# First experts: weights as the stationary operand, 256 gathered rows as the moving one

## The reference, cut to what matters

```python
logits = xf @ router_w + router_b                 # 4096 tokens, 4 experts
probs = softmax(logits)
top_p, top_i = top_k(probs, 2)                    # two experts for each token
gates = top_p / sum(top_p), scattered to [T, 4]
h = silu(einsum('td,edf->etf', xf, w1)) * einsum('td,edf->etf', xf, w3)   # D 256, F 1024
expert_out = einsum('etf,efd->etd', h, w2)
out = einsum('te,etd->td', gates, expert_out)
```

## Time and profile before

| | |
|---|---|
| median of 3 runs | 1969.44 us (1968.93 to 1970.89) |
| the profiled execution | 1968.24 us |
| its span in the trace | 1966.5 us |
| TensorE busy | 1695.0 us, 86% of the span |
| VectorE, GpSimd, ScalarE busy | 1152.6, 1051.4, 861.2 us |
| first experts, from the first `turn` to the copy of the last `down` | 514.18 to 1117.03 us |

### The profile page before, as it was taken

How to read it: one execution, slowest core, us unless ns; L and a number is a source line. 1 busy time by engine, 2 the same in 40 slices (tenths; PEclk the granted TensorE clock), 3 DMA queues, 4 the chain that set the end, 5 groups by cost and what they waited for, 6 DMA issues and landing times.

```text
span 1966.5 us, 32279 instructions
## 1 busy us (share of the span) xinstructions
PE 1695.0 (86%) x11144; PEld 1031.1 (52%) x11144; DVE 1152.6 (59%) x1838; ACT 861.2 (44%) x1932; POOL 1051.4 (53%) x871
## 2 busy tenths in 40 slices
PE   5699999977899999999999747788879676999992
PEld 3355555554466666666666523334434244677771
DVE  7799888976423232323323396999999986122224
ACT  3444444325344444443444356444444344444443
POOL 3377777623133333332444399999997954223322
PEclk8699999985799999999999967999999875999995
DMA  5012233106432233223343340011111355111115
GB/s 215 1 43 97 97 107 108 44 16 224 163 94 85 82 95 95 91 76 95 95 158 100 121 128 1 1 38 36 29 26 56 113 171 180 39 41 44 44 39 177
DMA packets 114424, 170.48 MB, mean 87 GB/s; under 512 B 27985, under 2 KB 78177, under 8 KB 114145
## 3 DMA queue, kind: packets, MB, share of 16 engines
q1 hardware_dynamic: 104096, 140.61, 21.1%
q0 software_dynamic: 10176, 27.80, 5.4%
HBM read 105.19 MB, written 63.18 MB: 86 GB/s over the span
## 4 chain that ended last, share of the span: by engine, by line
PE 64%; DVE 14%; POOL 10%; issue 6%; DMA 3%; ACT 3%; SPq 0%; DVEq 0%; POOLq 0%; ACTq 0%
PE ps L657 56%; POOL BIG L2014 9%; DVE BIG L1139 7%; PE ps L928 5%; DVE BIG L1596 2%; ACT BIG L1661 1%; PE ps L900 1%; DMA BIG<-YT 1%; DVE X L1139 1%; DVE bnst L1146 1%; DMA HB<-BIG 1%; PE ps L772 1%; POOL BIG L2135 1%; PE ps L832 1%; POOL X L2014 1%
## 5 line engine op out<-in xcount | busy, mean ns | idle before, releaser
L657 PE MATMUL ps<-BIG 128*128 (+9 forms) x8100 | 1301.8, 336 | 132.9 <-DVE BIG L1574 45.5
L657 PEld LDWEIGHTS ps<-BIG 128*128 128x128 f16 (+2 forms) x8100 | 739.1, 104 | 603.8 <-issue 114.9
L2014 POOL TENSOR_TENSOR BIG<-BIG 128x512 f16<-128x512 f32 (+5 forms) x530 | 765.4, 1478 | 261.2 <-ACT BIG L1661 242.3
L1139 DVE TENSOR_TENSOR BIG<-ps,BIG 128x512 f32<-128x512 f32 (+4 forms) x693 | 464.3, 724 | 271.1 <-ACT BIG L1661 225.4
L1661 ACT ACTIVATE BIG<-ps 128x512 f16<-128x512 f32 (+5 forms) x1036 | 396.7, 440 | 514.0 <-PE ps L657 264.8
L2109 POOL DMA_INDIRECT YT<-BIG x106 | 105.1, 992 | 541.8 <-ACT BIG L1661 541.8
L1139 DVE TENSOR_TENSOR BIG<-BIG,ps 128x512 f32<-128x512 f32 (+1 forms) x204 | 120.9, 597 | 414.7 <-PE ps L657 399.1
L1661 ACT ACTIVATE BIG<-BIG 128x512 f16<-128x512 f32 (+2 forms) x321 | 197.0, 630 | 133.4 <-DVE BIG L1139 98.8
L1815 ACT ACTIVATE BIG<-ps 128x512 f32<-128x512 f32 x212 | 126.8, 598 | 135.1 <-PE ps L657 135.1
L1596 DVE TENSOR_REDUCE BIG<-BIG 128x160 f32<-128x2560 f32 x64 | 183.5, 2868 | 0.0
L2104 POOL DMA_INDIRECT BIG<-HB,BIG x106 | 103.2, 974 | 69.7 <-DVE BIG L1139 43.7
(11 more groups left out here) (129 smaller groups left out, 857.6 us busy)
## 6 DMA issues: line engine op xcount, KB each, us to landing
WD<-BIG SPq DMA_DIRECT2D x112, 256.0 KB, 2.3
BIG<-in_v SPq DMA_DIRECT2D x32, 512.0 KB, 5.1
BIG<-WD SPq DMA_DIRECT2D x32, 512.0 KB, 5.0
BIG<-in_w SPq DMA_DIRECT2D x24, 512.0 KB, 3.9
BIG<-WD SPq DMA_DIRECT2D x32, 384.0 KB, 7.5
BIG<-YT SPq DMA_DIRECT2D x24, 512.0 KB, 4.9
HB<-BIG SPq DMA_DIRECT2D x64, 128.0 KB, 2.3
X<-in_x SPq DMA_DIRECT2D x4, 1024.0 KB, 11.7
```

Of the source, the lines that this page charges most:

```text
L657: return e.matmul(o, lhsT, rhs, start=start, stop=stop, skip_group_check=True)
L1139: return e.tensor_tensor(o, a, b, op)
L2014: return e.tensor_tensor(o, a, b, op)
```

## The change

In the first layer's experts, groups of 256 rows take the place of tiles of 128: 8192 / 256 + 3 = 35 groups (`NG`), which is 70 tiles of 128 for gathers, scatters and the down product. `up(j, g)` makes 256 inner features (two blocks of 128) for 256 rows in one bank: the weight's 128 columns are the stationary operand, at the register's address, and the 256 turned rows in `HTT` are the moving one. Inner features come out on partitions, so `turn_up` is gone: ScalarE's `up_hi` and VectorE's `up_lo` make the f16 pair straight from `UP` in SBUF. `UP` is now two buffers of 512 and `up` number u waits for `up_lo` of u - 2. `HIN` has four buffers, both gathers of a group are fetched before it, and the turned rows are copied 1024 wide. The second layer's experts keep their form (the code is split in two functions).

```diff
-                self.NS = CH * NT + E - 1
+                self.rows = 256 if l == 0 else 128
+                self.NG = CH * NT * 128 // self.rows + E - 1
+                self.NS = self.NG * self.rows // 128
...
-                self.HIN = area.ring(3, 2 * D, dt=f16)
-                self.HTT = area.ring(2, 4, 128, dt=f16)
-                self.UP = area.ring(2, 1024)
-                self.UPT = area.pairs(1 if l else 2, 8, 128)
+                self.HIN = area.ring(3 if l else 4, 2 * D, dt=f16)
+                self.HTT = area.ring(2, 4, self.rows, dt=f16)
+                self.UP = area.ring(2, 1024 if l else 512)
+                self.UPT = area.pairs(1 if l else 2, 8, self.rows)
...
-            return j - 25
+            return j - 25 if j - 25 < N_CV[1] else None
...
+            def first_experts():
+                m_ = M[0]
+                def turn(j):
+                    if j >= 2:
+                        pe.wait_ge(s["hTc"], j - 1)
+                    for t in (2 * j, 2 * j + 1):
+                        pe.wait_ge(ld_hi[t % 4], 16 * (t // 4 + 1))
+                        for k in range(4):
+                            m = e.transpose(bank_pair(6 + j % 2)[:, k, 128 * (t % 2):128 * (t % 2) + 128],
+                                            m_.HIN[t % 4][:, k * 128:(k + 1) * 128], ident16[:, :])
+                    m.then_inc(s["tn_ps"], 1)
+                def up(j, g):
+                    u = 4 * j + g
+                    for w, freed in enumerate(("su", "um")):
+                        idx = 2 * u + w
+                        if u >= 2:
+                            pe.wait_ge(s[freed], u - 1)
+                        pe.wait_ge(s["hTc"], j + 1)
+                        for blk in range(2):
+                            for k in range(2):
+                                for p, (a, b) in enumerate(HALVES):
+                                    m = mm(ps[idx % 4][:, 256 * blk:256 * blk + 256],
+                                           weight(0, j, a, 2048 * w + 1024 * k + 256 * g + 128 * blk, 128), m_.HTT[j % 2][:, 2 * b + k, :],
+                                           blk == 0 and k == 0 and p == 0, k == 1 and p == 2)
+                        m.then_inc(s["up_ps"], 1)
+                def down(t):
...
+                        pe.wait_ge(s["ut_lo"], 4 * j + n // 2 + 1)
...
+                for j in range(m_.NG):
+                    if j + 1 < m_.NG:
+                        reg(0, j + 1)
+                    up(j, 0)
+                    up(j, 1)
+                    if j:
+                        down(2 * j - 2)
+                        down(2 * j - 1)
+                    if j + 1 < m_.NG:
+                        turn(j + 1)
+                    up(j, 2)
+                    up(j, 3)
+                down(m_.NS - 2)
+                down(m_.NS - 1)
...
+                def up(u):
+                    act.wait_ge(s["up_ps"], 2 * u + 1)
+                    if u >= 2:
+                        act.wait_ge(s["ut_lo"], u - 1)
+                    e.activation(m_.UP[u % 2], ps[2 * u % 4][:, :], ACT.Silu).then_inc(s["su"], 1)
+                def up_hi(u):
+                    j, g = u // 4, u % 4
+                    act.wait_ge(s["um"], u + 1)
+                    if j >= 2:
+                        act.wait_ge(s["dn_ps"], 2 * j - 2)
+                    copy(m_.UPT[j % 2][0][:, 2 * g:2 * g + 2, :].rearrange(FLAT), m_.UP[u % 2]).then_inc(s["ut_hi"], 1)
...
+            def first_experts():
+                m_ = M[0]
                 for r in range(4):
-                    pool.wait_ge(st_hb[r], slot_base[l]["hb"] + 128)
+                    pool.wait_ge(st_hb[r], 128)
+                for t in range(4):
+                    fetch(0, t)
+                for j in range(m_.NG):
+                    for t in (2 * j, 2 * j + 1):
+                        if convert_at(t) is not None:
+                            convert(1, convert_at(t))
+                        if j and t % 2 == 0:
+                            put(0, t - 2)
+                            put(0, t - 1)
+                    for t in (2 * j + 4, 2 * j + 5):
+                        if t < m_.NS:
+                            fetch(0, t)
```

More of the change, by code:

```diff
@@ L866, in routing @@
                         m.then_inc(s["mp_ps"], 1)
[L868 to L880, removed]
+            regs = {}
@@ L903, in up @@
                 def up(j, hf):
[L904 to L918, removed]
+                    if j >= 2:
+                        pe.wait_ge(s["su"], at(l, "su") + 2 * (j - 2) + hf + 1)
+                    pe.wait_ge(s["hTc"], at(l, "hTc") + j + 1)
+                    for k in range(2):
+                        for p, (a, b) in enumerate(HALVES):
+                            m = mm(ps[(2 * j + hf) % 4][:, :], m_.HTT[j % 2][:, 2 * a + k, :],
+                                   weight(l, j, b, 1024 * k + 512 * hf, 512), k == 0 and p == 0, k == 1 and p == 2)
+                    m.then_inc(s["up_ps"], 1)
                 def turn_up(j):
@@ L975, in tensor @@
             routing(0)
-            experts(0)
+            first_experts()
             def merge_tick(t):
@@ L1491, in up_lo, with second_experts @@
+            def second_experts():
+                l, m_ = 1, M[1]
+                ut = m_.UPT[0]
+                dve.wait_ge(s["rt"], rt_at[l, "yi"])
+                for k in range(4):
+                    dve.wait_ge(st_hb[k], slot_base[l]["hb"] + 128)
+                for j in range(m_.NS):
                     for q in range(2):
@@ L1844, in experts @@
                     if j:
-                        down(j - 1)
-                    if l == 0 and convert_at(j) is not None:
-                        convert(1, convert_at(j))
+                        down(l, j - 1)
                 up_hi(NS - 1)
-                down(NS - 1)
+                down(l, NS - 1)
             def combine(i):
@@ L2118, in experts, with second_experts @@
+            def second_experts():
+                for r in range(4):
+                    pool.wait_ge(st_hb[r], slot_base[1]["hb"] + 128)
+                fetch(1, 0)
+                fetch(1, 1)
+                for j in range(M[1].NS):
+                    if j + 2 < M[1].NS:
+                        fetch(1, j + 2)
                     if j:
-                        put(j - 1)
-                    if l == 0 and convert_at(j) is not None:
-                        convert(1, convert_at(j))
-                put(NS - 1)
+                        put(1, j - 1)
+                put(1, M[1].NS - 1)
```

222 lines of the change are left out of this document (133 added, 89 removed).

## The result

The changed kernel takes 1942.12 us (median of four runs, 1939.68 to 1942.93) against 1969.18 for the kernel before in the same series: a ratio of 0.9864, 95% interval [0.9845, 0.9883], so 27.1 us less where 30.6 were forecast. Two later series of the same two kernels gave 0.9865 and 0.9877 (experiment 7), 25.6 and 24.5 us less.

What follows compares the result with a forecast made beforehand. TensorE's issue time in the first experts was taken as the bound. Terms -30.5 (matmuls, transposes, padding) + 1.3 - 0.9 (start) - 1.0 (end) + 0.5 (routing) gave -30.6 us, so 1938.8 us; range 1933 to 1956.

Steps and rivals of the forecast that it cites:

- what bounds: First experts: TensorE's issue time bounds the stage; period 16.16 us a group of 256 rows, 30.5 us less in all.
- the transposes and the narrow matmuls: First experts: fp32 transposes gone, 58.6 us off TensorE; 48 narrow matmuls a tile for 24 wide, 3.9 us on.
- start and end: First experts: first `up` 1.3 us later, a wait after it gone, -0.9; shorter wait at the last `down`, -1.0.
- the queue: Rival: TensorE's queue, with 82 sums and a register load a group, becomes the bound; up to 37 us more, chance 0.07.
- exposed or pacing loads: Rivals in `up`: weight loads exposed, 329 us more at full price, chance 0.08; or loads pace narrow matmuls, 107 us, 0.01.
- the subtraction: First experts: VectorE's step after the multiplication and ScalarE's copy, priced at 0.69 us.
- the loop's 2.7 us to spare: Silu, multiply, copy, subtract take 2.5 us, leaving 2.7 before `down`; rival that this loop replaces TensorE as bound, chance 0.03.
- later stages as long as before: Sign to look for: the stages behind the first experts, not changed, take the same time; difference 0.
- the routing: Ahead of the first experts: handles 70 columns for 67, +0.5 us, 0.7 at most.

Runs made afterwards that it cites:

- experiment 7: The changed kernel run again, unaltered, in two later series against the kernel before: 1944.44 us (ratio 0.9865) and 1943.13 us (0.9877).
- Experiment 1: The kernel before without its eight fp32 transposes a tile (`down` then multiplies other numbers): 1914.39 us, ratio 0.9708 to the kernel before.
- experiments 4 and 6: 4: changed kernel with groups of 128 rows, 2139.8 us. 6: changed kernel with 114 address sums a group, 1994.66 us, or 210 with matmuls halved, 2437.37 us.
- experiment 3: The changed kernel with expert 0's weights at constant addresses, so no register load or address sums in the first experts: 1945.78 us, one run.
- (2): The changed kernel with each `up` matmul cut into two of 128 rows with the same weights: 1958.81 us, ratio 0.9938 to the kernel before.

## Why the prediction was right, and what it missed

- *Right: what bounds.* The period, with TensorE busy throughout, was forecast at 16.16 us and is 16.217. The pace was 0.1095 instead of 0.1092: with the transposes 35 x 0.057 = 2.0 us less gain.
- *Right: the transposes and the narrow matmuls.* Experiment 1 gives 0.873 us a tile for 0.875. The sustained spacings of the Trainium skill (TensorE: Matmul & The Clock Gate, Back-to-back issue gap), 81 ns at 128 columns and 131 at 512, agree with no run here: it was 56 ns at 128, 109 at 256, 216 at 512. These fit the formula that the section gives for an isolated matmul, and that the prediction calls the one for a single stream.
- *Right: start and end.* The second gather puts off the first `up` by 1.3 us, as forecast. The end saved more: 0.36 us are left where 0.7 were expected. The first half group also ran 0.7 us nearer its full pace. It took 7.04 us for 48 x 0.1095 = 5.26, at a granted clock of 0.76 over it; before, have 7.71 for 24 x 0.216 = 5.18, at 0.69. The clock rose only during this piece in both kernels: from 440 us to its start the granted clock was 0.50 (1.2 GHz), with TensorE at work for 53 of the first 74 us and then for 0.6 of the last 2, and behind it, up to 532 us, it was 1.00 (2.4 GHz). The prediction had no term for it.

```profile
515.85:523.50 7.65, 7.65 (x26) 3.14 (x27) 0.69 (x1) 2.13 (x3) 0.00 (x0) 0.69 0.00 1
```

```profile
516.07:523.10 7.03, 7.03 (x51) 5.64 (x52) 1.38 (x2) 3.52 (x5) 0.00 (x0) 0.76 0.01 2
```

- *Right, and narrower than it looked: the queue.* Its upper bound for a sum, 0.126 us, was no bound: the price is 0.131 to 0.133, since the 0.025 us that it took off for each matmul are not there. By experiments 4 and 6 a group's register work is 82 x 0.131 + 0.65 = 11.4 us of 16.2, hidden under 256 columns a matmul. The prediction's bound added 0.025 us for each matmul and 3.1 for the register load, and so came to 17.2: the matmuls' part and most of the load's were not there. The forecast took 0 for all of it, and that held. With 128 columns the same work is 11.4 of 8.2 us and sets the pace: the swap alone is 170 us slower than before. The group of 256 rows is what makes it pay.
- *Rejected: exposed or pacing loads.* 3360 loads at register addresses take 97 ns, taking the register away (3) leaves the period as it is, and halving the matmuls (2) gives no pace near the load's 98 ns.
- *Wrong size, off the path: the subtraction.* It was priced at 0.69 us, as in the earlier trace rows; both its operands now are in SBUF, and it took 0.935 in the mean, 1.55 beside GpSimd's conversion. The timeline of VectorE, then GpSimd:

```profile
841.05 0.69 DVE L1199 TENSOR_TENSOR BIG<-BIG 128x512 f16<-128x512 f32 x1 [0.69 <-ACT BIG L1730]
...
843.69 1.55 DVE L1199 TENSOR_TENSOR BIG<-BIG 128x512 f16<-128x512 f32 x1 [0.70 <-ACT BIG L1730]
```

```profile
842.55 2.14 POOL L2121 TENSOR_TENSOR BIG<-BIG 128x1024 f16<-128x1024 f32 x1 [7.09 <-ACT BIG L1730]
```

  The long one starts inside the conversion and ends 0.55 us after the conversion does. The Trainium skill (SBUF — State Buffer, SBUF: two separate sides) says that a VectorE operation with two inputs in SBUF and a GpSimd operation that reads SBUF exclude each other for a whole instruction; these rows agree. Of the loop's 2.7 us to spare it took 0.86 where it fell, so TensorE never waited.
- *The step that failed: "later stages as long as before".* The merge lost 1.9 us in the profiles shown (2 to 3 in all), by the place of the buffers; that is shown. Of the other 4.3 us behind, 2.8 fell in the stretch to the second layer's gather, which scatters by 6.7 us over the kernels, and the rest in the last stage. Their cause is not settled, and no run here separates it from scatter.
- *Right in kind, a little small: the routing.* From its first row maximum to the first gather's issue it took 29.17 us before and 29.91 in the changed kernel, 0.74 more for +0.5. The rows, before and then after:

```profile
479.87 0.29 DVE L1351 TENSOR_REDUCE BIG<-BIG 128x32 f32<-128x128 f32 x1
509.04 1.20 POOL L2104 DMA_INDIRECT BIG<-HB,BIG  x1 [27.41 <-DVE BIG L1139]
```

```profile
478.04 0.29 DVE L1411 TENSOR_REDUCE BIG<-BIG 128x32 f32<-128x128 f32 x1
507.95 1.20 POOL L2210 DMA_INDIRECT BIG<-HB,BIG  x1 [28.13 <-DVE BIG L1199]
```

  The other kernels divide by the count of tiles: 29.18 to 29.22 us in the three with 67, 29.90 to 29.95 in the nine with 70. What made the table's first row -1.1 lies ahead of the routing: its first row maximum comes anywhere from 478.0 to 481.7 us over the kernels, and in this profile at the earliest.

The sum again, with the measured sizes: -30.6 + 2.0 (pace) - 1.3 (start and end, by the table's third row) + 0.2 (routing) + 2 to 3 (merge) = -27.7 to -26.7, where the three series have -27.1, -25.6 and -24.5. Up to some 3 us stay open, behind the merge or in the scatter.

## What to carry to other kernels

In a stretch where TensorE never waits, the distance between starts, times the count of matmuls, forecasts the gain to a few tenths of a per cent of the stage. When an operand that is addressed by a register becomes the one that changes with every matmul, count the address sums against the matmuls' columns first: here 0.13 us a sum with two sums for three matmuls, free under 256 columns and the bound at 128. And compare unchanged stages in the trace too, since a change that only shifts buffers can make them slower.

## What the runs showed of the hardware

- A sum on an address register costs TensorE's queue 0.13 us (experiments 4 and 6), and a register load from SBUF some 0.65 us where nothing covers it; in the changed kernel both are hidden (experiment 3).
- GpSimd's addition of 128 x 256 f32 takes 0.64 us in the median with its buffers 5 or 9 words past a multiple of 16, and 0.72 at 15 or 0 words past it. Only these four places were tried, and why is open.
